# A new start-up order, a root taken on ScalarE, and re-cut placement tables in an attention kernel

## What is computed

```python
x = x + tanh(g_xattn) * attention(layernorm(x), ctx, ctx)     # 16 heads, softmax over 1601 keys
x = x + tanh(g_ffn)   * moe(layernorm(x))                     # 8 experts, the top 2 for each token
# attention, for each batch b and head h:
#   q = layernorm(x) @ Wq[h];  k = ctx @ Wk[h];  v = ctx @ Wv[h]
#   out = softmax(q @ k.T * 0.125) @ v;  concat over heads @ Wo.T
# moe: softmax router, renormalised top 2, gelu(x @ w1.T + b1) @ w2.T + b2 for each chosen expert
```

## Time and profile before

| | us |
|---|---|
| median of three executions | 1292.09 |
| the profiled execution | 1290.77 |
| its span in the trace | 1289.0 |
| PE / DVE / ACT / POOL busy | 1244.2 / 1116.9 / 1084.3 / 553.5 |
| unit 0 starts on PE | 36.56 |

### The profile page before, as it was taken

The page is one execution under the profiler, slowest core; times in us unless marked ns, Lnnn a source line. Parts: engine busy times, 40 slices in busy tenths (PEclk is TensorE's granted clock), DMA queues, the critical chain, the costliest instruction groups (busy, mean ns, idle before and its releaser), DMA issues.

```text
span 1289.0 us, 42176 instructions
## 1 busy us (share of the span) xinstructions
PE 1244.2 (97%) x16259; PEld 623.0 (48%) x16259; DVE 1116.9 (87%) x1980; ACT 1084.3 (84%) x2196; POOL 553.5 (43%) x1213
## 2 busy tenths in 40 slices
PE   7999999999999999999999999999999999999992
PEld 2344444444444444444444444444444444499992
DVE  8899999999999999999999999999999999356434
ACT  2788998999898989899999999999999898866661
POOL 6324344353536262726252635445353512146542
PEclk9999999999999999999999999999999999999996
DMA  3332222212121212121212121222211110288886
GB/s 95 91 92 65 67 78 60 69 55 75 48 79 47 80 48 80 45 87 38 80 44 71 54 71 59 66 65 62 68 56 42 51 43 6 96 257 245 262 270 239
DMA packets 61092, 112.93 MB, mean 88 GB/s; under 512 B 13053, under 2 KB 36477, under 8 KB 60749
## 3 DMA queue, kind: packets, MB, share of 16 engines
q1 hardware_dynamic: 54187, 97.98, 25.9%
q0 software_dynamic: 4320, 8.99, 2.0%
q10 hardware_dynamic: 2385, 3.27, 0.7%
HBM read 52.77 MB, written 13.71 MB: 52 GB/s over the span
## 4 chain that ended last, share of the span: by engine, by line
PE 82%; SPq 6%; POOL 4%; DVE 3%; issue 2%; DMA 2%; ACT 0%; POOLq 0%; DVEq 0%
PE pv L911 31%; PE st L820 17%; PE mxp L874 13%; PE st L797 7%; PE st L1130 5%; PE mxp L1140 5%; SPq L415 4%; DVE mx L1679 2%; POOL kf L658 1%; PE mxp L881 1%; POOL ksp L663 1%; PE st L941 1%; POOL rows L722 1%; PE mxp L847 1%; DVE x_sb L1872 1%
## 5 line engine op out<-in xcount | busy, mean ns | idle before, releaser
L1679 DVE TENSOR_REDUCE mx<-mxp 128x2 f32<-128x1024 f32 x768 | 916.9, 1218 | 43.2 <-PE mxp L874 35.9
L1169 ACT ACTIVATE arena<-st 128x512 f32<-128x512 f32 (+1 forms) x1664 | 883.6, 597 | 64.4 <-PE st L820 50.1
L911 PE MATMUL pv<-arena 128*32 128x256 f32 x6656 | 531.6, 391 | 0.6 <-ACT pv_sb L1176 0.3
L820 PE MATMUL st<-qpack,kpack 51*128 51x256 bf16 (+1 forms) x3328 | 486.9, 272 | 3.0 <-DMA qpack<-mxT 2.6
L874 PE MATMUL mxp<-kpack,qpack 48*128 48x512 bf16 x1502 | 406.1, 383 | 1.5 <-DVE mx L1679 1.5
L820 PEld LDWEIGHTS st<-qpack,kpack 51*128 51x128 bf16 (+1 forms) x3328 | 192.4, 95 | 279.2 <-ACT arena L1169 153.1
L911 PEld LDWEIGHTS pv<-arena 128*32 128x32 f32 x6656 | 131.2, 108 | 173.8 <-issue 104.1
L689 POOL CAST mxs<-nmx 128x8 bf16<-128x8 f32 x64 | 12.2, 191 | 345.1 <-DVE nmx L1689 345.0
L874 PEld LDWEIGHTS mxp<-kpack,qpack 48*128 48x128 bf16 x1502 | 121.1, 93 | 68.5 <-issue 34.1
L1332 ACT ACTIVATE arena<-st,bias 128x256 f32<-128x256 f32 (+1 forms) x172 | 74.9, 437 | 46.2 <-PE st L1130 42.0
L732 POOL DMA_INDIRECT results<-ysb,idx x71 | 68.2, 961 | 79.9 <-DVE ysb L1814 54.2
(11 more groups left out here) (202 smaller groups left out, 983.7 us busy)
## 6 DMA issues: line engine op xcount, KB each, us to landing
kpack<-ksp SPq DMA_DIRECT2D x756, 50.0 KB
arena<-in_w12T SPq DMA_DIRECT2D x43, 576.0 KB
arena<-in_ctxT SPq DMA_DIRECT2D x15, 800.5 KB, 4.7
qpack<-qsp SPq DMA_DIRECT2D x187, 32.0 KB
xblk<-rows SPq DMA_DIRECT2D x28, 132.0 KB, 4.0
rows<-in_pads SPq DMA_DIRECT2D x8, 264.0 KB
arena<-results SPq DMA_DIRECT2D x8, 256.0 KB, 7.0
arena<-results ACTq DMA_DIRECT2D x8, 256.0 KB, 7.1
```

The lines of the kernel that those rows point to most:

```text
L820: ins = eng.matmul(ring[i][0:n, jj * N:(jj + 1) * N], kpack[rows, b % 2, g * JJ + jj, kt * P:kt * P + n], qpack[rows, b % 2, g * JJ + jj, ...
L911: ins = eng.matmul(pv[32 * j:32 * j + 32, 0:N], vaug[0:n, b % 2, kt, at:at + 32], pt[0:n, (2 * u + rg) % PT_BUFS, jj * N:(jj + 1) * N], st ...
L1169: eng.activation(pt[0:n, c % PT_BUFS, :], ring[bank_of["S", u, p]][0:n, :], ACT.Exp, scale=SCALE).then_inc(s_exp, 1)
L1679: eng.tensor_reduce(mx[:, tj, w, :], src[:, :, 0:WIN], AX.X, ALU.max).then_inc(s_red, 1)
```

## The change

The diff does the following.

- **The root of batch 0.** ACT takes a square root (table function Sqrt), VectorE its reciprocal, and one Newton round is left instead of three. An Exp of a single column behind it brings back the table for exponentials. The memsets of `rank`, `taken` and `ge`, and three of the normalisation steps of batch 1, move from before the first maxima to between them.
- **The front's order.** The identity is loaded from ACT's queue. Batch 1's rows, the value weights and batch 1's context are loaded from SP's queue at the start (the context was loaded at the end of the front). TensorE turns the rows behind one key chunk instead of two, and makes the last key chunk behind the first pair. Key packs of groups 0 and 1 are issued by kind.
- **Pairs and values.** 19 pairs run before unit 0 (18 before), of which 15 are fp32 (18 before). Five value chunks (four of batch 0 and one of batch 1) run before unit 0, behind pairs 14, 15, 16 and 18; before, it was one. The other three chunks of batch 1 go to units 0, 6 and 15; before, chunks 1 to 3 of batch 0 were at units 1, 6 and 7, and the four chunks of batch 1 at places 25 to 30.
- **A wait moves.** Before a batch's new keys overwrite `ksp`, somebody must wait for the packs that read it: this was ACT's `first_keys`, and is now POOL's `split_keys`. ACT now waits for POOL's last read of `kf` instead.
- **Tables.** LEAD is 21 instead of 23, and the tables of places are new. The turn of the heads moves from place 3 to 2, routing from 26 to 31, the query product from 42 to 45.
- **ORDER.** In the last three expert blocks the large one goes first.

```diff
--- before.py
+++ after.py
+ORDER[-3:] = [ORDER[-2], ORDER[-3], ORDER[-1]]
 PHASES = [(0, FULL, SL), (FULL, LARGE - FULL, SL), (LARGE, NBK - LARGE, SS)]
 K_AT = {1: 0, 4: 1, 5: 2, 8: 3}
-V_AT = {25: 0, 26: 1, 27: 2, 30: 3}
-HEADS_AT = 3
-TURN_AT, PLACE_AT = {8: 1, 22: 2, 31: 3, 47: 4}, {9: 1, 23: 2, 31: 3, 49: 4}
-POST_AT = {7: "C", 9: "F", 21: "L", 23: "R"}
-X_AT, Q_AT = 36, 42
-FIRST_K_AT = {8: 0, 9: 1, 10: 2, 17: 3}
+V_AT = {24: 0, 26: 1, 27: 2, 35: 3}
+HEADS_AT = 2
+TURN_AT, PLACE_AT = {8: 1, 22: 2, 31: 3, 47: 4}, {9: 1, 22: 2, 31: 3, 50: 4}
+POST_AT = {7: "C", 9: "F", 22: "L", 23: "R"}
+X_AT, Q_AT = 37, 45
+FIRST_K_AT = {2: 0, 7: 1, 15: 2, 18: 3}
 RANK_AT, LAST_RANK_AT, COUNT_AT, PLAN_AT = 46, 35, 38, 40
-L_NORM_AT, X_NORM_AT = 10, 23
-LOGITS_AT, EXP_AT, ROUTE_AT = 24, 26, 26
+L_NORM_AT, X_NORM_AT = 10, 25
+LOGITS_AT, EXP_AT, ROUTE_AT = 24, 26, 31
 ROWS_AT, LAST_ROWS_AT = {1: 40, 2: 42, 3: 44}, {9: 0, 10: 1, 11: 2, 12: 3}
-FIRST, LEAD = 18, 23
-WINDOWS_AT = ("0111111121010111101011111110111110110111101111111101",
-              "0000100001000000010001000010000010010000100000000001")
-FIRST_WINDOWS_AT = ("0100201010210011010100000110111100010011000111211000",
-                    "1110002020001000010120201020001021011001110000000111")
+FIRST, LEAD = 19, 21
+WINDOWS_AT = ("0111111121110111111000112001111110110110001100111000",
+              "0000100000000000001110001100000010010001100110000111")
+FIRST_WINDOWS_AT = ("1100010001110111000201100000110100011010100010011000",
+                    "0102012110010000021100202010010111001000111101000111")
 PER_BATCH = NG * NMX
-EARLY = FIRST
+EARLY = NMX + 2
 EARLY_HEADS = -(-EARLY // NMX) * JJ
-FIRST_V, FIRST_TURN = 5, 14
-FIRST_V_AT, FIRST_X_AT, FIRST_Q_AT = {1: 1, 6: 2, 7: 3}, 3, 5
+FRONT_V, FIRST_TURN = {14: 1, 15: 1, 16: 1, 18: 2}, 14
+FIRST_V_AT, FIRST_X_AT, FIRST_Q_AT = {0: 5, 6: 6, 15: 7}, 0, 4
+FIRST_NEWTON = 1
 ISSUED, FIRST_ISSUED = [[sum(int(at[q][r]) for r in range(UNITS) for q in range(2) if 2 * r + q < c)
                          for c in range(2 * UNITS)] for at in (WINDOWS_AT, FIRST_WINDOWS_AT)]
...
 
+def front_values(n):
+
+    done = sum(FRONT_V[k] for k in FRONT_V if k < n)
+    return range(done, done + FRONT_V[n])
+
+
 def rank_at(b):
...
         return "K", b + 1, keys_at(b)[r]
-    if b + 1 < B and r in V_AT:
+    if 0 < b < B - 1 and r in V_AT:
         return "V", b + 1, V_AT[r]
...
-    take("V", 0, 0)
-    take("M", 0)
+    for n in range(FIRST):
+        if n == FIRST_TURN:
+            take("M", 0)
+        if n in FRONT_V:
+            for c in front_values(n):
+                take("V", *divmod(c, NV))
     for u in range(B * UNITS):
         b, r = divmod(u, UNITS)
         take("S", u, 0)
...
             eng.dma_start(ctx_sb[:, 0, HALF:M], ctxT[0][:, HALF:M]).then_inc(s_ctx_b, 16)
-            eng.dma_start(id_sb[:, :], ident).then_inc(s_id, 16)
+            eng.dma_start(x_sb[:, NT:2 * NT, :], xs[:, 1, :, :]).then_inc(s_x1, 16)
+            eng.dma_start(wv_sb[:, :], wv).then_inc(s_wv, 16)
+            eng.dma_start(ctx_sb[:, 1, :], ctxT[1]).then_inc(s_ctx[1], 16)
 
             def pack_keys(b, g, kinds=range(PARTS)):
...
+            eng.wait_ge(s_kone, 1)
+            ones_rows(0)
+            first_keys_high(eng, 0, 0)
             first_query_rows(eng, range(PARTS), 0)
             first_query_rows(eng, range(PARTS - 1, PARTS), 1)
-            first_keys_low(eng, 0)
-            other_keys(eng, 1, 0)
-            eng.wait_ge(s_kone, 1)
-            ones_rows(0)
+            first_keys_high(eng, 1, 0)
+            first_keys_low(eng, 0, 0)
+            first_keys_low(eng, 1, 0)
             eng.wait_ge(s_mxT, 1)
             place_half(eng, 0, 0)
             for rg in range(RG):
                 other_keys(eng, 2, rg)
-            eng.dma_start(ctx_sb[:, 1, :], ctxT[1]).then_inc(s_ctx[1], 16)
             pack_keys(0, 3)
             eng.dma_start(wo_sb[:, :], woT).then_inc(s_w2, 16)
...
                     eng.wait_ge(s_khi, NK * b + c + 1)
+                    if c == 0:
+                        for g in range(NG):
+                            eng.wait_ge(s_kd[(b - 1) % 2][g], 16 * PACKS * ((b - 1) // 2 + 1))
                     eng.tensor_copy(ksp[:, 0, cols], kf[:, cols]).then_inc(s_pool, 1)
                     steps += 1
...
-                if m == 0 and rg == 0:
-                    if G == 0:
-                        eng.wait_ge(s_qearly, JJ)
-                    else:
-                        eng.wait_ge(s_qlater, EARLY_HEADS - JJ)
+                if pair < 2 and rg == 0:
+                    eng.wait_ge(s_qearly, pair + 1)
+                if pair == NMX and rg == 0:
...
                     eng.wait_ge(s_khi, NK)
-                if b == 0 and g == 0:
-                    eng.wait_ge(s_v, next(c for c, (t0, tn) in enumerate(VCH) if kt < t0 + tn) + 1)
-                elif r == 0:
+                if r == 0:
                     eng.wait_ge(s_v, NV * (b + 1))
...
             eng.wait_ge(s_wk, 16)
-            for c in range(NK - 2):
-                keys(0, c)
+            keys(0, 0)
             eng.wait_ge(s_id, 16)
             turn_rows("X", 0)
-            keys(0, NK - 2)
+            keys(0, 1)
             eng.wait_ge(s_wq, 16)
             queries(0)
-            keys(0, NK - 1)
-            for n in range(issued(0, 0)):
+            keys(0, 2)
+            for n in range(FIRST):
                 maximum(*divmod(n, NMX))
-                if n == FIRST_V:
+                if n == 0:
+                    keys(0, 3)
                     eng.wait_ge(s_wv, 16)
-                    values(0, 0)
-                elif n == FIRST_TURN:
+                if n == FIRST_TURN:
                     turn_maxima(0)
+                if n in FRONT_V:
+                    for c in front_values(n):
+                        values(*divmod(c, NV))
             for u in range(B * UNITS):
                 b, r = divmod(u, UNITS)
                 scores(u, 0, windows(u, 0)[:1])
...
                     src = ring[bank_of["K", b, c]]
-                    if c == 0:
-                        for g in range(NG):
-                            eng.wait_ge(s_kd[(b - 1) % 2][g], 16 * PACKS * ((b - 1) // 2 + 1))
-                        if b == 1:
-                            eng.wait_ge(s_mxp, RG * EARLY)
+                    eng.wait_ge(s_k3, NK * (b - 1) + c + 1)
+                    if b == 1 and c == 0:
+                        eng.wait_ge(s_mxp, RG * EARLY)
                 else:
                     src = k0p[c]
...
             eng.dma_start(x_sb[:, 0:NT, :], xs[:, 0, :, :]).then_inc(s_x0, 16)
+            eng.dma_start(id_sb[:, :], ident).then_inc(s_id, 16)
             eng.dma_start(wq_sb[:, :], wq).then_inc(s_wq, 16)
-            eng.dma_start(wv_sb[:, :], wv).then_inc(s_wv, 16)
-            eng.dma_start(x_sb[:, NT:2 * NT, :], xs[:, 1, :, :]).then_inc(s_x1, 16)
+            eng.wait_ge(s_var0, 1)
+            eng.activation(tmp[:, :], var[:, :], ACT.Sqrt).then_inc(s_root0, 1)
+            eng.wait_ge(s_id, 16)
+            eng.activation(warm[:, :], id_sb[:, 0:1], ACT.Exp)
             first_keys(0, 0)
+            copy_rows(0)
+            first_keys(0, 1)
             first_high(0)
-            first_keys(0, 1)
-            copy_rows(0)
+            first_keys(0, 2)
             first_high(1)
-            first_keys(0, 2)
+            first_queries(0)
             first_keys(0, 3)
-            first_queries(0)
-            for c in range(2, NK):
-                first_high(c)
-            eng.wait_ge(s_id, 16)
+            first_high(2)
+            first_high(3)
+            first_keys_high(eng, 0, 1)
             eng.activation(id_bf[:, :], id_sb[:, :], ACT.Copy).then_inc(s_idb, 1)
             for h in range(JJ, EARLY_HEADS):
                 later_queries(h)
-            first_keys_high(eng, 1)
             first_query_rows(eng, range(PARTS - 1), 1)
-            copy_values(0, 0)
-            first_keys_low(eng, 1)
-            other_keys(eng, 1, 1)
-            copy_maxima(0)
-            eng.wait_ge(s_mxT, 1)
-            place_half(eng, 0, 1)
+            first_keys_high(eng, 1, 1)
+            first_keys_low(eng, 0, 1)
+            first_keys_low(eng, 1, 1)
+            for n in range(FIRST):
+                if n == FIRST_TURN:
+                    copy_maxima(0)
+                    eng.wait_ge(s_mxT, 1)
+                    place_half(eng, 0, 1)
+                if n in FRONT_V:
+                    for c in front_values(n):
+                        copy_values(*divmod(c, NV))
             for u in range(B * UNITS):
                 b, r = divmod(u, UNITS)
...
                     own += NT
+                elif n == 2 and norm_no[kind, b] == 0:
+                    eng.wait_ge(s_dve, own)
+                    eng.tensor_scalar(var[:, :], stat[:, :, 1], LN_EPS, None, ALU.add
+                                      ).then_inc(s_var0, 1)
...
                 eng.wait_ge(s_dve, own)
-                if n < 4 * NEWTON:
```

(34 more changed lines are left out.)

23 lines of the change are left out of this document (12 added, 11 removed).

## The result

The changed kernel takes 1304.38 us (median of 7 runs, 1298.14 to 1306.22). The kernel before took 1292.19 us (7 runs) on the same occasions. The ratio on record is 1.0066, 95% interval 1.0041 to 1.0091; the quotient of the two medians is a little more, 1.0094. The profiled execution took 1298.14 us, the shortest of the seven; its span is 1296.1 us, against 1289.0 before. So the trace can account for 7.1 us, and not for all of the 12.2 between the medians. Lines of the changed kernel are numbered some 12 to 30 higher: L1407, L1412 and L1417 are the variance step, the halving and the guess of the root that stood at L1380, L1385 and L1390.

A forecast was written before the change was run, and what follows sets the result against it. TensorE was taken to set the end from unit 0 on, VectorE close behind. Terms 0.5 + 3.3 + 0.3 + 1.3 = 5.4 us took the profiled 1290.77 to 1285.4, the median to 1286.7; range 1280 to 1292.5.

The forecast's parts named there:

- What bounds the kernel: Whole kernel: TensorE sets the end, working some 66.3 of 67.7 us in a steady batch, with VectorE close behind at 64.04.
- Start of unit 0: Front: a shorter root and earlier maxima start unit 0 at 36.0 instead of 36.56, 0.5 us gained (-0.5 to 1.3).
- Values moved, pairs, moved wait in batch 0: Batch 0: value chunks made before unit 0 save 3.3 us, pairs 0.3, ACT's wait for key packs going to POOL 1.3.
- The wait at unit 26: Batch 0: TensorE's 1.31 us wait for the DMA placing a maximum stays; 0 taken, bounds -1.5 and 1.3.
- PLACE_AT 50: Placing the next batch's maxima at unit 50 instead of 49: the prediction gave it no term of its own.
- The steady tables and the lead: Steady batches: same work, LEAD changes nothing while TensorE never waits for a placed maximum; 0 a batch, bounds -0.4 and +0.4.
- Rival A: Steady batches: the new tables also remove waits, 0.4 us a batch, giving 1281.1 us; chance 0.18.
- Rival B: Batch 0: another wait, for the placing DMA at unit 26 or VectorE, replaces TensorE's; gain only 1.1, 1291.0 us; chance 0.18.
- Rival C: Steady batches: the routing mask comes too late, TensorE waits 0.6 to 0.9 us at place 46; 1297.2 us; chance 0.12.
- The sign that I had named for C: Steady batches: a wait of the rank product for POOL, and a distance over 68.3 us between `pv_sb` copies.
- Rival D: Front: the table switch for the root drains ACT too, making first queries and unit 0 1.4 us later; 1288.1 us; chance 0.05.
- The tail: Last expert blocks: a large and a small one swap places with equal work; 0, within 0.5 us.

The follow-up runs named there:

- z4: The changed kernel with the fifth maxima placed at 49 and, on GpSimd, the split of the group's maxima moved behind the second key columns: 0.9994 of the kernel before.
- z1: The kernel before with the fifth maxima placed at 50 instead of 49 and nothing else: 0.9998 of the kernel before.
- x1: The changed kernel with one number changed, the next batch's maxima placed at unit 49 instead of 50: 1.0067 of the kernel before.
- x2: The changed kernel with placing at 49 and all steady tables (windows and places) of before, LEAD still 21: 1.0152 of the kernel before.
- v1: z4 with the scatters of the third and fourth part of the rows moved behind all key splits on GpSimd: 1.015 of the kernel before.
- a0: The changed kernel itself, unaltered, on another chip: 1.0122 of the kernel before.
- w1: x1 a second time, on a chip where the kernel before takes 1293 us: 1.0037 of the kernel before.

## Why the prediction was wrong, point by point

- **What bounds the kernel.** TensorE sets the end, I wrote, with VectorE "close behind". Right, but I drew nothing from the second half. The chain in the earlier trace rows gave VectorE 3%; with 0.7 us of hold a batch it is 13%, and with the new tables the distance grows by as much as the hold.
- **Start of unit 0.** I forecast the product 1.4 us earlier (1.83 measured), the first maximum at 11.5 (10.71), the 13th at 28.6 (27.26), unit 0 at 36.0 (35.11). The mechanism was right, the term too small: 1.45 instead of 0.5. The 2.4 us that I took for the first maximum didn't follow from my own terms, which give 1.4 + 1.44 - 1.45 = 1.4; it measured 3.15. The small instructions between the maxima delayed them by 0.67 + 0.07 + 0.16 = 0.9 us (from the start of each, at 13.71, 15.51 and 16.74, to that of the next reduction), not the 1.8 that I took. One of them was held as well: `half` at 13.71 lasted 0.75.
- **Values moved, pairs, moved wait in batch 0** (3.3, 0.3 and 1.3). With the pause at unit 52 taken away, in z4, the value product of unit 53 starts at 106.62 against 111.88: 5.3 us ahead, where the whole sum was 5.4. Of this the start of unit 0 gives 1.1 (35.50 against 36.56), so the three terms together are 4.2 and not 4.9. That the moved wait had also to cover a chunk six units earlier, worth over 8 us, I didn't see.
- **The wait at unit 26**, taken at 0: no wait there that is longer than 0.34. Right.
- **PLACE_AT 50.** The failed step of batch 0: I costed it at nothing and named no work that hides it. I did not look at what SyncE issues between places 49 and 50. It costs 4.6 to 4.8 us here, and nothing where unit 52 comes later (z1).
- **The steady tables and the lead**, "LEAD changes nothing while TensorE never waits for a maximum to be placed". This is the step that failed, and it made the sign. The lead also says when a group's last pair is reduced, and GpSimd takes that result in program order, ahead of key splits. I took 0 with 0.4 a batch either way; it was +0.67. I had followed VectorE and TensorE past the change, and not GpSimd's queue.
- **Rival A** (new tables remove waits): they do, 0.8 per cent against the old ones at lead 21 (x1 and x2), but they are waits that this lead makes. **Rival B**: the pause does move to the next placing DMA, not at unit 26 but at unit 52. **Rival C** forecast slower, but not by what happened: the mask came at 445.02, GpSimd's addition 0.25 us later, and the rank product at 445.68 without a wait. The sign that I had named for C, a distance over 68.3, did come (68.35); its cause did not.

```profile
445.02 0.17 DVE L1523 TENSOR_TENSOR mask<-oh,cw 128x16 bf16<-128x16 f32 x1
...
445.27 0.20 POOL L721 TENSOR_TENSOR before<-before,mask 128x8 bf16<-128x8 bf16 x1 [1.62 <-DVE mask L1523]
...
445.68 0.19 PE L814 MATMUL st<-mask,tri_bf 128*32 128x16 bf16 x4
```

- **Rival D**: the activation behind the load starts 0.02 us after it. No drain is seen, against the Trainium skill, page "ScalarE: Activation LUTs", section "What ACT_TABLE_LOAD costs"; here the measurement decides.
- **The tail**, taken at 0 within 0.5: the stretch behind the last copy became 1.3 us shorter. The same stretch varies by more between runs of one kernel on different chips, so I claim nothing from it.

## What to carry to other kernels

A number that says how far one stream runs ahead sets not only whether its consumer waits. It sets when each result falls due in every engine that handles it, and in an in-order queue all that stands behind that result moves with it: follow each queue, that of the half-idle engine too. When two engines are nearly full, a delay of a few tenths on the second can go into the period in full: here 0.68 us of hold and 0.67 of period. And a table that was cut for one lead should be changed together with it, or not at all.

## What the runs showed of the hardware

- VectorE's TENSOR_SCALAR of 2 elements a row takes 0.16 us alone and ends 0.02 to 0.03 us behind a TENSOR_TENSOR of GpSimd that was running when it began: 0.46, 0.56, 0.75, 0.88 us, whatever was left. A CAST of GpSimd does the same: in the kernel before `var` took 0.20 us beside one, at 468.93. VectorE's reductions of `mxp` beside the same operations keep their 1.22 us. GpSimd's DMA_INDIRECT doesn't hold it: in v1 the step took 0.17 us with 0.62 us of one still to run. The Trainium skill, page "SBUF — State Buffer", section "Who interferes with whom", has the rule: the two engines share a port pair under an exclusive lock, and `tensor_scalar` can want it while `tensor_reduce` never does. The traces agree.
- Behind a pause of TensorE of 1.66 us the granted clock was 0.50 from 108 to 112 us, with TensorE full, and it was back at 1.00 from 114 on. It fell in both traces of the changed kernel (in a0 it was 0.60 from 108 to 110 and 0.50 to 114) and not at unit 52 of w1, x1 and z1, which have no such pause. A pause doesn't settle it, though: w1 and x1 both have one of 0.94 us, ending at 65.08 and 64.96, and behind it the clock was 0.62 and 0.53 in w1 (66 to 68, 68 to 70 us) and 1.00 in x1.
- Chips differ in the experts' layers. The kernel before started its last value product at 1120.02 and 1122.87 us on two of them, and its span at 1289.0 and 1303.7; from 1200 to 1240 us the DMAs moved 276 GB/s on the one and 241 on the other.
